# Four-layer graph and expert network: second biases of the first two expert layers moved into the gap before the first gathered tile

## What is computed

```python
x = x + gnn(layernorm(x), adj)
xf = layernorm(x)
w = dense [1024, E] matrix, two nonzero weights per row (top 2 of the gate)
y = sum over e of w[:, e] * (act(xf @ w1[e] + b1[e]) @ w2[e] + b2[e])
x = x + y        # layer 0: x + layernorm(xf + y) * gamma + beta
```

## Time and profile before

| | us |
|---|---|
| median of 3 runs | 1093.96 |
| lowest, highest | 1091.34, 1099.96 |
| the profiled execution: time | 1096.7 |
| the profiled execution: span, first to last instruction | 1094.8 |
| its mean granted TensorE clock | 0.926 of full |

### The profile page before, as it was taken

One profiled execution on the slowest core, in us unless ns is written; L12 is line 12 of the kernel. 1 busy time (PEld: TensorE's weight loads), 2 busy tenths in 40 slices (PEclk: granted clock), 3 DMA queues, 4 the chain that ended last, 5 costly groups with the idle time before them and its releaser, 6 DMA issues. The chain is left out here.

```text
span 1094.8 us, 22761 instructions
## 1 busy us (share of the span) xinstructions
PE 956.3 (87%) x7554; PEld 896.3 (82%) x7554; DVE 701.8 (64%) x1653; ACT 514.7 (47%) x1001; POOL 445.4 (41%) x470
## 2 busy tenths in 40 slices
PE   6884999896899589989989899999889985999992
PEld 5584999786888579978979899999758875999992
DVE  3786777666899557776544466655656864666664
ACT  1252777134666357712045577767234532444341
POOL 1152577426776147621200145551244521344441
PEclk8797999798999789979989999999899995999997
DMA  7007865300000437322450011168200007655954
GB/s 250 2 25 241 312 219 178 97 1 1 11 10 11 183 109 269 135 83 95 129 195 8 16 35 38 38 220 308 92 2 5 11 21 268 255 168 172 322 162 135
DMA packets 57675, 132.30 MB, mean 121 GB/s; under 512 B 9664, under 2 KB 35712, under 8 KB 52864
## 3 DMA queue, kind: packets, MB, share of 16 engines
q1 hardware_dynamic: 47376, 106.45, 27.7%
q0 software_dynamic: 9024, 24.65, 7.4%
q10 hardware_dynamic: 1200, 0.23, 0.1%
HBM read 191.97 MB, written 17.56 MB: 191 GB/s over the span
## 5 line engine op out<-in xcount | busy, mean ns | idle before, releaser
L1959 PE MATMUL r_pH<-e_xsT,e_w 128*128 128x128 f32 x2304 | 281.5, 280 | 10.0 <-DVE e_xsT L2072 5.0
L1959 PEld LDWEIGHTS r_pH<-e_xsT,e_w 128*128 128x128 f32 x2304 | 272.4, 197 | 12.8 <-issue 9.6
L1914 POOL DMA_INDIRECT y_rows<-e_ys,e_to x94 | 156.8, 1668 | 190.6 <-DVE e_ys L2102 95.5
L1924 POOL DMA_INDIRECT e_xs<-xn_rows,e_idx x94 | 103.4, 1100 | 161.7 <-DVE e_idx L2076 120.4
L2088 DVE TENSOR_TENSOR e_w_lo<-e_w,e_w_hi 128x1024 fp32r<-128x1024 f32 (+1 forms) x74 | 113.4, 1532 | 13.8 <-ACT e_w_hi L2030 12.7
L1974 PE MATMUL r_pY<-e_w_hi,e_h_hi 128*128 128x256 f32 x384 | 114.5, 298 | 2.2 <-issue 2.2
L2030 ACT ACTIVATE e_w_hi<-e_w 128x1024 fp32r<-128x1024 f32 (+1 forms) x74 | 96.0, 1298 | 27.7 <-DMA e_w<-w_in 22.4
L498 ACT ACTIVATE g_t<-g_g,g_small 128x1024 f32<-128x1024 f32 x56 | 64.1, 1150 | 94.8 <-POOL g_small L485 94.8
L1974 PE MATMUL r_pY<-e_w_lo,e_h_hi 128*128 128x256 f32 x384 | 108.4, 282 | 0.0
L1974 PE MATMUL r_pY<-e_w_hi,e_h_lo 128*128 128x256 f32 x384 | 108.4, 282 | 0.0
L451 DVE SCALAR_TENSOR_TENSOR g_lm<-g_g,g_small,g_t 128x1024 f32<-128x1024 f32 x56 | 71.6, 1280 | 9.5 <-ACT g_t L498 7.0
(11 more groups left out here) (321 smaller groups left out, 1970.6 us busy)
## 6 DMA issues: line engine op xcount, KB each, us to landing
e_w<-w_in SPq DMA_DIRECT2D x56, 1024.0 KB
e_w<-w_in SPq DMA_DIRECT2D x84, 512.0 KB
e_w<-w_in SPq DMA_DIRECT2D x52, 514.0 KB
e_w<-w_in SPq DMA_DIRECT2D x24, 1028.0 KB
e_w<-y_rows SPq DMA_DIRECT2D x32, 256.0 KB, 5.4
p_adj<-adj_in SPq DMA_DIRECT2D x8, 512.0 KB, 11.3
xn_rows<-xn SPq DMA_DIRECT2D x32, 128.0 KB, 1.7
n_adjT<-adjT_in SPq DMA_DIRECT2D x8, 512.0 KB, 4.9
```

What stands on the lines that cost most here:

```text
L1914: pool.indirect_dma_start(out=y_rows[:, :], in_=ys[b][:, :], in_offset=None, out_offset=bass.IndirectOffsetOnAxis(ap=to[b][:, :], axis=0))\
L1924: pool.indirect_dma_start(out=xs[b][:, :], out_offset=None, in_=xn_rows[:, :], in_offset=bass.IndirectOffsetOnAxis(ap=idx[b][:, :], axis=0))\
L1959: ins = nc.tensor.matmul(pH[b % 2][:, f, :], w1[b][:, at:at + P], xsT[b % 2][:, c, :], start=(c == 0), stop=(c == DC - 1))
```

## The change

For layers 0 and 1 (`gap`) the bias work leaves the end of the layer and goes between the table and the first gathered tile:

- VectorE makes the weights and the dense matrix ahead of the table's rows (`vector_weights` ahead of `rows`) and, after the destinations, adds the bias in four pairs of row tiles, 512 values wide.
- TensorE turns all eight row tiles behind the table, into the four PSUM tiles pT and pY, and sums pair by pair into the two pH tiles. The second pair waits until the table's rows are read (they lie in one of the pH tiles), the third and fourth for the additions of the first and second. The 56 fillers behind the table are gone.
- ScalarE copies each turned pair ahead of its loop.
- The first two `rise` wait for the additions of the last pairs (`clear`).
- SyncE loads `b2` ahead of the expert weights instead of behind them.
- At the end TensorE waits for `tiles_over`, a memset that VectorE does behind the last tile's copy, where it waited for the last bias addition.

In layer 2 (`own`) the order stays as it was. The core of the diff:

```diff
+            def vector_weights(dve):
+                link = links[0]
                 dve.wait_ge(exped, 1)
...
+        class GapBiases:
...
+            def turn(self, pe):
+                pe.wait_ge(self.ready, 1)
+                for n in range(NT // DC):
+                    for part in range(DC):
+                        ins = nc.tensor.transpose(self.pT[n][0:self.E, part * P:(part + 1) * P], self.rows[:, n * DC + part, :],
+                                                  ident[:, :])
+                    ins.then_inc(self.turned, 1)
...
+            def sum(self, pe, rows_known):
+                pe.wait_ge(self.loaded, 16)
+                for pair in range(NT // 2):
+                    pe.wait_ge(self.kept, pair + 1 if pair < NT // 2 - 1 else NT // DC)
+                    if pair == 1:
+                        pe.wait_ge(rows_known, 1)
+                    if pair >= 2:
+                        pe.wait_ge(self.added, pair - 1)
+                    for t in (2 * pair, 2 * pair + 1):
+                        ins = nc.tensor.matmul(self.pS[pair % 2][:, t % 2, :], self.turned_rows[:, t * P:(t + 1) * P],
+                                               self.b2[:, :], start=True, stop=True)
+                    ins.then_inc(self.summed, 1)
+
+            def clear(self, pe, b):
+                pe.wait_ge(self.added, NT // 2 - 1 + b)
+
+            def add(self, dve, target):
+                for pair in range(NT // 2):
+                    dve.wait_ge(self.summed, pair + 1)
+                    two = slice(2 * pair, 2 * pair + 2)
+                    nc.vector.tensor_tensor(target[:, two, 0:D], target[:, two, 0:D], self.pS[pair % 2][:, :, :], ALU.add)\
+                        .then_inc(self.added, 1)
...
+                    if gap:
+                        biases.load(sp)
                     for b in range(UN):
...
                         if not early(i, b, 2):
                             pe.wait_ge(h_ready, t - 1)
+                        elif gap:
+                            biases.clear(pe, b)
...
                         ranks(pe)
                         table_of_pairs(pe)
+                        if gap:
+                            biases.turn(pe)
+                            biases.sum(pe, rows_known)
                     last = loop(pe, step)
-                    if biases:
+                    if own:
                         pe.wait_ge(biases.ready, 1)
                         biases.turn(pe, 0)
...
+                    if gap:
+                        pe.wait_ge(biases.tiles_over, 1)
                     after.tensor(pe)
...
                         slots(act)
                         column(act)
+                        if gap:
+                            biases.keep(act)
                     loop(act, step)
...
-                        for part in (slots, tiles, columns, rows, first_rows, experts_known, destinations):
+                        for part in (slots, tiles, columns, weights, rows, first_rows, experts_known, destinations):
                             part(dve)
+                        if biases:
+                            biases.add(dve, after.base)
                     last = loop(dve, step)
...
                     end(last, UN - 1)
+                    if gap:
+                        nc.vector.memset(more[:, :], 0).then_inc(biases.tiles_over, 1)
```

More of the change, by code:

```diff
@@ L1667, in gate @@
             return ((tensor_ranks, tensor_table), (scalar_exps, scalar_slots, scalar_column),
-                    (vector_onehots, vector_slots, vector_tiles, vector_columns, vector_rows, vector_experts, vector_dest),
+                    (vector_onehots, vector_slots, vector_tiles, vector_columns, vector_weights, vector_rows, vector_experts,
+                     vector_dest),
                     tiles_known, rows_known, turns_known)
@@ L1712, in add, with __init__, load, keep @@
                                             self.pT[t % 2][:, :, :].rearrange("p c q -> p (c q)"), ALU.add).then_inc(self.added, 1)
+        class GapBiases:
+            def __init__(self, ph, E, name, pT, pY, pH):
+                self.E, self.name = E, name
+                self.pT = [t[:, :, :].rearrange("p c q -> p (c q)") for t in pT] + [t[:, :] for t in pY]
+                self.pS = [h[:, :, :].rearrange("p f q -> p (f q)").rearrange("p (t d) -> p t d", d=D) for h in pH]
+                self.rows, self.turned_rows = ph.sb("dense", [P, NT, E]), ph.sb("denseT", [E, N])
+                self.b2 = ph.sb("b2", [E, D])
+                self.ready, self.turned, self.kept = ph.sem("dense_ready"), ph.sem("dense_turned"), ph.sem("dense_kept")
+                self.loaded, self.summed, self.added = ph.sem("b2_loaded"), ph.sem("bias_summed"), ph.sem("bias_added")
+                self.tiles_over = ph.sem("tiles_over")
+            def load(self, sp):
+                sp.dma_start(self.b2[:, :], A[self.name][0:self.E, :]).then_inc(self.loaded, 16)
+            def turn(self, pe):
[5 more added lines that the diff above has]
+                    ins.then_inc(self.turned, 1)
+            def keep(self, act):
+                for n in range(NT // DC):
+                    act.wait_ge(self.turned, n + 1)
+                    nc.scalar.activation(self.turned_rows[:, n * DC * P:(n + 1) * DC * P], self.pT[n][0:self.E, :], ACT.Copy)\
+                        .then_inc(self.kept, 1)
+            def sum(self, pe, rows_known):
[18 more added lines that the diff above has]
+                        .then_inc(self.added, 1)
@@ L1804, in experts @@
                 room = [h[:, :, :].rearrange("p f q -> p (f q)") for h in (pT if own_loaded else pH)]
-                biases = SecondBiases(pr, E, b2_name, pT) if b2_name else None
+                gap = b2_name and not own_loaded
+                biases = GapBiases(pr, E, b2_name, pT, pY, pH) if gap else SecondBiases(pr, E, b2_name, pT) if b2_name else None
                 gate_tensor, gate_scalar, gate_vector, tiles_known, rows_known, turns_known = \
-                    gate(pr, L, E, all_probs, un, function, None if own_loaded else pY[1][:, 0:P], room, biases)
+                    gate(pr, L, E, all_probs, un, function, None if own_loaded or gap else pY[1][:, 0:P], room, biases)
                 w1 = [ph.sb(f"w1{n}", [P, W1C]) for n in range(UN)]
@@ L1877, in _ @@
                         sp.dma_start(w2[b][:, :], w2_v[guess(b), :, :]).then_inc(w2_loaded[b], 16)
-                    if biases:
+                    if biases and not gap:
                         biases.load(sp)
@@ L2119, in first_rows @@
                             next_rows(b, b)
-                    onehots, slots, tiles, columns, rows, experts_known, destinations = gate_vector
+                    onehots, slots, tiles, columns, weights, rows, experts_known, destinations = gate_vector
                     onehots(dve)
@@ L2124, in _ @@
                             for part in {0: [slots, own.split_weights], 1: [tiles], 2: [columns, experts_known],
-                                         5: [rows, first_rows, destinations]}.get(k, []):
+                                         5: [rows, first_rows, destinations, weights]}.get(k, []):
                                 part(dve)
```

## The result

| | before | after |
|---|---|---|
| median, executions | 1094.59 us, 12 | 1088.38 us, 12 |
| lowest, highest | 1090.56, 1099.96 | 1083.42, 1090.73 |
| the profiled execution: time, span | 1096.7, 1094.8 | 1088.6, 1086.7 |
| mean granted clock | 0.926 | 0.917 |

The ratio is 0.994 with a 95% interval of 0.992 to 0.996: 6.2 us less. I had forecast 1.6 us more.

A forecast was written before the change was run, and what follows sets the result against it. TensorE, busy 87% of the span, was taken as the bound. Terms -2.0 + 0.8 (ways out of layers 0, 1) + 2.3 + 0.5 (their gaps) = +1.6 us: 1095.6 against 1093.96 us, range 1090.5 to 1099.0.

The forecast's parts named there:

- That load needs 5.5 us to land, so the data was there at 206.7: Layer 0's way out: first load of sorted results, issued at 201.22, lands 5.5 us later; part of a 2.0 us gain.
- the 1.3 and 0.8 that I left to the additions: Ways out of layers 0 and 1: time in us by which the bias additions held the first weighted sum.
- The last `fall` 0.7 us earlier: Layer 0's way out: without two transposes and a copy wait, the last `fall`, its store and load come 0.7 us earlier.
- the 0.3: Layer 1's way out: the last `fall` moves 0.3 us earlier, by the same steps as in layer 0.
- Layer 0's gap, +2.3: Wait for layer 0's first gathered tile: narrow bias products at the low clock delay TensorE's first product by 2.3 us.
- Rival A: Gaps of layers 0 and 1: bias work lifts the clock; sum -2.0 us, 1092.0 us; chance 0.17.
- Layer 1's gap, +0.5: Wait for layer 1's first gathered tile: rows and gather 0.5 us later, bias products fit just ahead of the gathered tile.
- Layer 1's way out, the clock takes back 1.9 where 1.1 is gained: Layer 1's end: sum starts 1.1 us earlier, but fillers run too early and the clock falls; net +0.8 us.
- Rival D: Ways out of layers 0 and 1: sums wait for stores, only layer 0's 0.7 us left; about +3 us; chance 0.05.

The follow-up runs named there:

- e10: Changed kernel with weights and dense matrix made right behind the slots, turned ahead of the table (layers 0, 1), and 112 + 48 + 36 fillers in layer 1's way out: 1085.31 us, 0.9924.

## Why the prediction was wrong, point by point

- *"That load needs 5.5 us to land, so the data was there at 206.7"*: this step failed. 5.5 us is the median of eight loads that are issued one behind the other within 4 us; the sum waits for the first, and that needs about 2.9 us. From issue to sum it was 2.7 to 3.1 us in 19 of the 22 stages of layers 0 and 1 that have no additions ahead of the sum, 3.5 to 4.0 in the other three. With this number the steps as written give 208.05 - (201.22 + 2.9) = 3.9 us for layer 0 and 3.5 for layer 1 in place of the 1.3 and 0.8 that I left to the additions. The trace of the kernel before could have told. These are its landings of L303 in layer 0's way out, of all eight (198 to 215 us) and of the first alone (201.2 to 201.3):

```profile
DMA to landing us min/median/max: 2.7/5.5/6.6
DMA to landing us min/median/max: 2.7/2.7/2.7
```

  So the data of the first sum was there at 203.9 and not at 206.7. Of the 4.15 us from there to the sum, 0.9 are the additions and 3.25 the folding and the copies behind them. Layer 3, which has no bias, shows the same:

```profile
1080.16 3.98 SPq L303 DMA_DIRECT2D e_w<-y_rows  x8
1082.90 0.48 DVE L307 SCALAR_TENSOR_TENSOR x<-e_w,wts,x 128x256 f32<-128x256 f32 x1 [5.95 <-DMA e_w<-y_rows]
```

  It is 2.74 us from load to sum.
- *The last `fall` 0.7 us earlier:* from the fourth gathered tile's turn to the load it was 85.5 and 84.3 us before, 85.3 and 83.9 after, 0.3 us less, which is within the scatter of the loop. The end of the stage tells more: from the end of the last split hidden tile (L2093, L2162 after) to the first load's issue it was 6.07 us in both profiles before and 5.57 in both after, and the `fall` starts 0.1 us behind that tile instead of 0.56. So 0.5 of the 0.7 us are shown, for the reason given. In layer 1 it was 6.06 and 5.93 before, 5.92 in both after: at most 0.1 of the 0.3.
- *Layer 0's gap, +2.3:* right, +2.5, for the reasons given (eight narrow products, then the last addition and the reading of the turns), with the clock at 0.50. I had the turns at 0.22 us each and the products at 0.85, 8.6 us in all; together they took 9.0.
- *Rival A,* that the gap's work lifts the clock, is refuted: in the changed kernel the granted clock stays at 0.50 under the products of both layers, and in the run with fillers ahead of the table it falls beneath those of layer 1. By the rule quoted from the Trainium skill's page "TensorE: Matmul & The Clock Gate", section "Part 1: The HAM clock gate", they should have lifted it; the windows decide, and for these products the rule does not hold.
- *Layer 1's gap, +0.5:* +0.2 by the first product in the first profiles, +0.1 by the second tile's in the means of two. The products do not fit ahead of the gather, as I had it: the turn follows them at once, and in the run with fillers ahead of the table the tile was turned 1.1 us earlier. Nor does the gather share a queue with the weight loads: it goes by q0, they by q1; what they share is the DMA engines.
- *Layer 1's way out, the clock takes back 1.9 where 1.1 is gained:* the mechanism was right and the give-back 2.3, shown by the run with fillers up to the first turn. Against a gain of 3.6 it could not turn the sign.
- *Rival D,* nothing gained at the ends: the opposite was the case.
- *What no step named:* layer 3, -2.0 us in two profiles. With the corrected terms the sum is -2.5, and -3.1 with the 0.6 us of the last `fall`, which would still have missed the 6.2 measured. Of the rest, -2.0 is placed there, its cause open; -1.1 is ahead of layer 0's gap, and chance as far as the profiles tell.

## What to carry to other kernels

When several loads are issued one behind the other, the median to landing tells little of the first. Ask the profile for the first one's landing alone, or take it from a place where its reader waits for nothing else, in this kernel the same stage of another layer. When a late step is taken away, look at what was queued behind it on other engines, since in layer 0 that was most of the gain. Work moved off the end of a stage takes TensorE's activity with it: look at what then stands idle, and bridge it with fillers that start at once, since late ones run at the low clock and hold the queue. Work for a gap is better put where TensorE waits for a table than between the table and the data: the profile shows the first tile 1.7 us earlier, though the time does not show it clear of the scatter.

## What was not expected of the hardware

Narrow f32 products (16 rows of weights by 256 columns) kept TensorE busy for 7 us and left the clock at 0.50, and in the run with fillers ahead of the table it fell from 1.00 to 0.50 beneath those of layer 1 (8 rows by 256), after they had run at 1.00 from 377.4 to 380.8.

The same work gets the clock back at very different times. In the attention of layer 1, which no edit touches, the changed kernel's second profile and e10's start alike; TensorE's rows of the one, then of the other:

```profile
255.43 1.97 PE L537 MATMUL g_tp<-ident,g_lm 128*128 128x128 f32 x8 [9.09 <-DVE g_lm L451]
...
259.53 2.06 PE L548 MATMUL g_o<-n_V,g_pT 128*128 128x65 f32 x16
```

```profile
252.71 1.97 PE L537 MATMUL g_tp<-ident,g_lm 128*128 128x128 f32 x8 [9.09 <-DVE g_lm L451]
...
256.82 3.51 PE L548 MATMUL g_o<-n_V,g_pT 128*128 128x65 f32 x16
```

The one has the clock at 1.00 within 258 to 262, 4 to 5 us after its first product, the other only within 268 to 270, 16 us after, though TensorE was busy 2.00 of 2.00 us from 256 to 268:

```profile
262.00:264.00 2.00, 2.00 (x12) 2.00 (x11) 2.00 (x4) 2.00 (x4) 1.94 (x2) 0.50 0.00 0
...
268.00:270.00 2.00, 2.00 (x18) 2.00 (x18) 1.58 (x3) 0.72 (x1) 0.27 (x1) 0.85 0.00 0
```

From the first sum of layer 0 to layer 1's `past` it is 173.0 us in the one that gets it late, against 169.4. Such differences are as large as the terms of this study. A short stretch around the changed place, compared between profiles, decides more than a whole layer or the medians.
